# One slot fewer for the experts, and eight more residual tiles loaded early

## The reference

```python
h = _layernorm(x) * (1 + ca) + sa
x = x + ga * attention(h)                       # 16 heads, causal, rotary
h = _layernorm(x) * (1 + cb) + sb
gate_scores = sigmoid(h @ Wg.T + balance_bias)  # 16 experts
topk_scores, topk_idx = top_k(gate_scores, 2)   # two different experts per token
topk_scores = topk_scores / (topk_scores.sum(-1) + 1e-6)
expert(e, h) = silu(h @ W1[e]) @ W2[e]          # 512 -> 256 -> 512
x = x + gb * sum(score * expert(e, h))
```

## Time and profile before

| | |
|---|---|
| median of 3 runs | 1680.94 us (1679.05 to 1681.72) |
| the profiled execution | 1677.18 us |
| its span | 1675.4 us |
| mean granted TensorE clock | 0.943 |
| PE busy | 1424.2 us, 85% |
| DVE busy | 1243.9 us, 74% |
| ACT busy | 835.5 us, 50% |
| POOL busy | 760.4 us, 45% |
| DMA | 255.07 MB, mean 152 GB/s |

### The profile page before, as it was taken

One profiled execution on the slowest core, in us unless ns is written; L12 is line 12 of the kernel. 1 busy time (PEld: TensorE's weight loads), 2 busy tenths in 40 slices (PEclk: granted clock), 3 DMA queues, 4 the chain that ended last, 5 costly groups with the idle time before them and its releaser, 6 DMA issues. The chain is left out here.

```text
span 1675.4 us, 27972 instructions
## 1 busy us (share of the span) xinstructions
PE 1424.2 (85%) x8739; PEld 1012.4 (60%) x8739; DVE 1243.9 (74%) x2932; ACT 835.5 (50%) x1418; POOL 760.4 (45%) x677
## 2 busy tenths in 40 slices
PE   5679998899899889999987998999873999999900
PEld 4556665566566556656655565665341999999800
DVE  3577777687777768777776776778757777777787
ACT  4324646634454763445465434555413666666522
POOL 3245355352434535243453433454525677777500
PEclk9799999999999999999999999999995999999955
DMA  6544444534344453434445342435644454444399
GB/s 211 173 155 151 133 132 102 164 114 158 101 129 126 112 163 114 157 95 133 125 114 164 114 158 90 121 86 164 228 151 167 160 184 157 144 150 141 121 346 382
DMA packets 128529, 255.07 MB, mean 152 GB/s; under 512 B 15632, under 2 KB 67344, under 8 KB 127904
## 3 DMA queue, kind: packets, MB, share of 16 engines
q1 hardware_dynamic: 104192, 184.46, 35.6%
q0 software_dynamic: 13952, 48.25, 8.6%
q10 hardware_dynamic: 10272, 20.97, 3.4%
HBM read 167.60 MB, written 86.02 MB: 151 GB/s over the span
## 5 line engine op out<-in xcount | busy, mean ns | idle before, releaser
L687 ACT ACTIVATE probs<-ring 128x1024 f32<-128x1024 f32 (+3 forms) x384 | 310.1, 811 | 187.7 <-PE ring L541 118.9
L506 PE MATMUL ring<-stack_t 96*128 96x512 f32 (+3 forms) x768 | 297.2, 411 | 24.1 <-DMA stack_t<-stack_dram 15.4
L484 PE MATMUL ring<-w_parts,h_hi 128*128 128x384 f32 x1024 | 275.2, 350 | 9.3 <-DVE neg_max L847 4.0
L1148 POOL TENSOR_TENSOR rope_a<-rope_a,rope_b 128x256 f32<-128x256 f32 x128 | 127.6, 997 | 337.6 <-DVE rope_b L920 337.6
L850 DVE CUSTOM_DVE_ANT_0 ring<-ring,later_b 128x384 f32<-128x384 f32 (+3 forms) x512 | 246.6, 496 | 23.6 <-PE ring L506 22.7
L506 PEld LDWEIGHTS ring<-stack_t 96*128 96x128 f32 x768 | 142.2, 193 | 173.8 <-issue 64.9
L1134 POOL TENSOR_TENSOR prob_sum<-prob_sum,probs 128x1024 f32<-128x1024 f32 (+3 forms) x128 | 229.9, 1796 | 22.8 <-ACT probs L687 21.9
L535 PE MATMUL ring<-stack_t 128*128 128x512 f32 (+3 forms) x768 | 212.6, 359 | 22.7 <-ACT probs L687 12.3
L484 PEld LDWEIGHTS ring<-w_parts,h_hi 128*128 128x128 f32 x1024 | 191.0, 197 | 17.6 <-issue 12.3
L847 DVE TENSOR_REDUCE neg_max<-ring 128x1 f32<-128x512 f32 x256 | 174.6, 682 | 13.5 <-PE ring L506 12.6
L484 PE MATMUL ring<-w_parts,h_lo 128*128 128x384 f32 x512 | 176.4, 345 | 0.0
(11 more groups left out here) (192 smaller groups left out, 2438.5 us busy)
## 6 DMA issues: line engine op xcount, KB each, us to landing
stack_t<-stack_dram SPq DMA_DIRECT2D x384, 128.0 KB, 3.3
stack_dram<-parts SPq DMA_DIRECT2D x64, 512.0 KB, 2.7
w_parts<-w_dram SPq DMA_DIRECT2D x24, 768.0 KB, 7.3
w_sb<-y_dram SPq DMA_DIRECT2D x32, 512.0 KB, 8.6
w_sb<-w SPq DMA_DIRECT2D x22, 512.0 KB, 5.6
x_in<-x SPq DMA_DIRECT2D x32, 256.0 KB, 3.8
x<-x SPq DMA_DIRECT2D x32, 256.0 KB, 3.5
x_dram<-x SPq DMA_DIRECT2D x32, 256.0 KB, 2.6
```

The source lines that it names most:

```text
L484: mm = nc.tensor.matmul(ring[:, BANK[use], 0:384], lhs[:, c, cols], rhs[:, c, :], start=(k == 0), stop=(k == len(products) - 1))
L506: nc.tensor.matmul(ring[:, BANK[use], 0:width], stack_t[0:MROW, i % 2, 0, h, qt * P:qt * P + P], stack_t[0:MROW, i % 2, 1, h, kc * 512:kc ...
L687: nc.scalar.activation(probs[:, step % PROBS, :, q0:QC], ring[:, bank:bank + 2, q0:QC], ACT.Exp)\
L1148: nc.gpsimd.tensor_tensor(rope_a[:, t % 2, :], rope_a[:, t % 2, :], rope_b[:, :], ALU.add)\
```

## The change

The expert stage runs over `USED` = floor(79.875) = 79 slots in place of `SLOTS` = 80. The tables of the routing keep 80 entries. The hardware loop of PE, ACT and DVE has 18 turns in place of 19 (bodies 4 to 75); bodies 76 to 78 stand unrolled behind it, and then the two that drain. POOL's program has one fetch and one send fewer.

Eight more residual tiles (`FREED`) are loaded in the expert stage: four into the W1 and W2 tiles of expert 0 once 32 slots have gone by `w2_lo`, and four into those of expert 1 once 64 have. (An expert can have at most 4096 pairs, 32 slots.) The last stage then loads 12 residual tiles in place of 20. Its `y_pair` buffers now lie over the W1 of experts 8 to 15, its `x_late` over the W2 of experts 8 and up.

```diff
+USED = (2 * B * L + E * (P - 1)) // P
...
-            EARLY = 12
+            EARLY, FREED = 12, 8
+            most = -(-B * L // P)
...
+            w1_tiles = w1_sb[:, :, :, :].rearrange("p e c f -> p (e c f)").rearrange("p (t d) -> p t d", d=D)
+            w2_tiles = w2_sb[:, :, :, :].rearrange("p e f d -> p (e f) d")
+            x_early += [tiles[:, 2 * e + n, :] for e in range(2) for tiles in (w1_tiles, w2_tiles) for n in range(2)]
...
-                    with eng.Fori(1, SLOTS // 4) as i:
+                    with eng.Fori(1, USED // 4) as i:
...
-                    for s in range(SLOTS, SLOTS + LAST):
-                        body(s, s % 4, range(s - SLOTS + 1, 4))
+                    for s in range(USED - USED % 4, USED):
+                        body(s, s % 4, range(4))
+                    for s in range(USED, USED + LAST):
+                        body(s, s % 4, range(s - USED + 1, 4))
...
-                        for s in range(SLOTS + LAG):
-                            if s < SLOTS:
+                        for s in range(USED + LAG):
+                            if s < USED:
...
-                            pool.wait_ge(y_out[k], 16 * (SLOTS // 4))
+                            pool.wait_ge(y_out[k], 16 * len(range(k, USED, 4)))
...
-                        sp.wait_ge(early_in, 16 * EARLY)
+                        for t in range(EARLY, EARLY + FREED):
+
+                            sp.wait_ge(w2_lo_r, most * ((t - EARLY) // 4 + 1))
+                            sp.dma_start(x_early[t], x1_dram[t, :, :]).then_inc(early_in, 16)
+                        sp.wait_ge(early_in, 16 * (EARLY + FREED))
...
-            y_pair = w1_sb[:, :, :, :].rearrange("p e c f -> p (e c f)").rearrange("p (t k d) -> p t k d", t=2 * DEPTH, d=D)
-            x_late = w2_sb[:, :, :, :].rearrange("p e f d -> p (e f) d")
+            EARLY += FREED
+            y_pair = w1_sb[:, E // 2:E, :, :].rearrange("p e c f -> p (e c f)").rearrange("p (t k d) -> p t k d", t=DEPTH, d=D)
+            x_late = w2_tiles[:, E:E + TT - EARLY, :]
```

## The result

The changed kernel took 1670.91 us (median of 6 runs, 1668.70 to 1673.64) against 1679.99 for the kernel before in the same comparison (6 runs, 1677.54 to 1685.61). The ratio is 0.9943, with a 95% interval of 0.9924 to 0.9962: 9.6 us less, between 6.4 and 12.8 (the two medians alone differ by 9.1). The forecast was 1673.6 us and a gain of 7.3 us. So the way was right, the measured gain is 2.3 us above the forecast, and the median of 1670.91 lies 0.2 us inside the low end of the range, 1670.7. The gain of 7.3 lies inside the interval.

The account below looks back on a forecast made before the run. PE was taken to bound the expert stage, DVE and then full DMA the last; 3.6 us from the slot plus 3.7 from the last stage made 7.3, so 1680.94 became 1673.6 us, range 1670.7 to 1677.3.

Parts of the forecast that it names:

- The slot in its own stage: Expert stage, bound by PE: one slot fewer saves one period, 3.61 us, and leaving the loop costs PE nothing.
- POOL's piece of "issue": A 3.57 us idle piece before a scatter in POOL's straight code, used to bound the unrolled bodies' cost by 3.6 us.
- The loads in the expert stage: Eight residual loads in two groups of four beside gathers and scatters: cost 0, bounded above by 5.2 us.
- The last stage: 12 late residual tiles in place of 20, eight loads or 2.10 MB fewer: gain 3.7 us, bounds 0 and 5.1.
- Way (b): Last stage: the pace of 2.55 us begins eight tiles later, at tile 25 in place of 17, gaining 3.5 us.
- part 1: 79 slots: gain one period, 3.61 us; work in the drain behind is the same, just earlier.
- (c): Last stage: ACT's lead over DVE grows to at most 3.8 us, worth 0.6 us; less than half taken, total 3.7.
- (a): Last stage: if DMA stayed full all the time, 2.10 MB at 411 GB/s would save 5.1 us.
- By bytes: Rival: last stage gains 5.1 us by bytes, with the slot 8.7 us in all, 1672.2 us; chance 0.15.
- The round trip: Rival: store and load latency sets the last stage's slow pace; total gain 3.6 to 5.1 us, about 1676.6; chance 0.12.
- The stall behind the loop: Rival: PE stalls up to 3.57 us in the unrolled bodies, eating the slot's gain; total 3.7, 1677.2 us; chance 0.07.
- the slower case: Rival: PE waits for code in each of three unrolled bodies, 10.7 us; 3.4 us slower, 1684.3; chance 0.03.

Follow-up runs that it names:

- `no_late_residual`: Changed kernel without the 12 residual loads of the last stage, early tiles added instead; last stage 74.46 us, 3.8 less than the changed kernel's first profile.
- `depth_12_late20`: 79 slots, 12 buffers in place of 8, but the 20 late residual tiles of before; ratio 0.9963 to the kernel before, last stage 80.04 us.
- the slot's two runs: 79 slots alone, with the 12 early residual tiles and buffer places of the kernel before; ratios 0.9989 and 0.9990 to that kernel.

## Why the prediction was right where it was, and where it was not

- **The slot in its own stage**: 3.61 us forecast. Over all profiles the expert stage is 283.2 to 283.5 us with 80 slots and 279.6 to 279.9 with 79: 3.6 us. Right, and no stall in the unrolled bodies. POOL's piece of "issue" was no measure for PE, and 3.57 us was too high a price for it. The scatter ahead of it in the kernel before began at 1570.48, so the next came 4.56 us later, 0.95 more than the period of 3.61.
- **The loads in the expert stage**: forecast at nothing. Right, and still right with the burst doubled.
- **The last stage**: forecast 3.7 for the loads. Without the slot's part they give 81.6 - 77.5 = 4.1 us, with it 82.0 - 79.1 = 2.9 (3.9 and 3.5 by the column "DVE"). Way (b), the slow pace eight tiles later, is near what happened: waits from tile 15 to 17 against 23 to 26. Of the changed kernel's 80.24 us, 1.7 lie ahead of tile 0, where the first load landed late.
- **The step that failed** is in part 1. I counted the slot as one period and what stands behind it as "the same work", "just earlier", so its effect on the last stage stood in the sum as nothing, without a reason. The runs show 0.5 us more in that stage with 20 late tiles and 1.6 with 12 (0.8 and 1.1 by the column "DVE", which leaves the late first load out). So the term for the last stage, 3.7, measured 81.6 - 79.1 = 2.4 us for the change as a whole, 2.8 by "DVE", and the sum of the stages 6.1 in place of 7.3. What in 79 slots makes the last stage longer stays open.
- **The lead in (c)** was misread as well. I had seen it grow by 0.3 us a tile from tile 8 to 11 and took 3.8 us as what eight buffers allow. But tiles 5 to 7 of the same trace stand at 3.7, held by ACT's own order, and with 12 buffers the limit is the same 3.7. Tile 8, the first into a freed buffer, is a drop to 2.4, so the growth is only the way back. From tile 12 to 20, with eight buffers and no residual loads, the lead went from 0.75 to 2.5 in the first profile of the change, and from 2.2 to 2.5 up to 3.4 to 3.7 in the other four: 0.1 to 0.2 us a tile. The step was worth only 0.2 us in the sum, and that the slow pace began at tile 25 or 26 in these four is near the "tile 25 or so" of the forecast partly by luck.
- **The reason against (a) was half right.** I wrote that no load removed from tiles for which DVE is the bound gives time. With 12 buffers it does: bytes taken away let DMA run ahead in that part, and 5.0 us comes. With eight 1 to 2 us of it is lost because DMA can't run ahead. ACT's order of stores, which also holds buffers longer, was not varied.
- **The rivals.** By bytes: not with eight buffers, and 5.0 us with 12. The price of 4.8 us cited beside it is by a fit that the Trainium skill ("DMA: Bandwidth & Descriptors", section "Anatomy of one DMA") gives for the GpSimd path, while SP issues these loads. The round trip: refuted by `no_late_residual` and by the 15.0 us of `depth_12_late20`. The stall behind the loop, and with it the slower case: not seen in any of the profiles.
- **The total.** The two stages give 6.1 us and the measured ratios say 9.6 and 7.9; the forecast was 7.3. The first interval, 6.4 to 12.8, just leaves out the 6.1, the second, 4.9 to 10.9, holds it. So that the whole time came out near the forecast is in part luck: the stages gave less than forecast, and 1.8 and 3.5 us of the measured 7.9 and 9.6 came from elsewhere. In the slot's two runs the whole gave less than the stages (1.8 and 1.7 us against 3.2). The unchanged part ahead varies by up to 9 us, which can do both, but no run separates chance from an influence of the changed program on that part. The forecast put it at nothing, and named 3.4 us as what a measurement can tell.

## What to carry to other kernels

When a stage is bound by DMA at its end and by an engine at its start, ask whether DMA is full in the part where it isn't the bound. A share of 0.98 with 357 GB/s was not full; the same engines moved 402 to 415 once they had buffers to load into. Here the bytes taken from the stage gave their full price (5.0 of 5.1 us) with 12 buffers, and 2.9 to 4.1 with eight, so count both together. When you read how far one engine leads another, ask first what holds the leader: here it was its own program order. And don't take the stage behind a change as the same just because its work is: compare it too. Where a change is worth less than the scatter of the code ahead of it, time the stage inside the trace, from a mark at its start to one at its end, and let the whole time only confirm it.

## What was not expected of the hardware

- The busy share of the DMA engines doesn't tell how full they are: 0.98 at 353 to 359 GB/s in the changed kernel, 1.00 at 358 and 0.98 at 374 in `no_late_residual`, and 1.04 at 410 to 415, all in the same stage.
- The same attention code reaches the expert stage at times up to 9 us apart (1305.26 to 1314.50 for the fourth `w_hi`), while the expert stage itself repeats within 0.3 us.
- One slot fewer in the expert stage made the last stage longer, by 0.8 to 1.1 us of DVE's part, in every profile. The cause isn't shown.
- A DMA share of 0.86 beside it left PE's period of 3.61 us untouched.
